# Linear attention: the summary's steps one slot later, and the keys' minimum on ScalarE

## The reference, cut to what matters

```
kvp = kv @ Wkv.T;  k, v = split(kvp)            # kv: 32 x 1500 x 256
q, k = phi(q), phi(k)                           # phi(x) = x + 1 if x > 0 else exp(x)
kv_summary = einsum('bhsd,bhse->bhde', k, v);   k_sum = k.sum(-2)
z = 1 / (einsum('bhld,bhd->bhl', q, k_sum)[..., None] + 1e-6)
attn = einsum('bhld,bhde->bhle', q, kv_summary) * z
out = attn * sigmoid(query @ Wg.T + bg) @ Wo.T
```

## Time and profile before

| | |
|---|---|
| median of three runs | 3338.97 us |
| the profiled execution's own time | 3340.39 us |
| its span in the profile | 3338.4 us |
| TensorE, VectorE, ScalarE, GpSimd busy over the span | 94%, 67%, 54%, 53% |
| mean granted TensorE clock | 0.97 of full |

### The profile page before, as it was taken

How to read it: one execution, slowest core, us unless ns; L and a number is a source line. 1 busy time by engine, 2 the same in 40 slices (tenths; PEclk the granted TensorE clock), 3 DMA queues, 4 the chain that set the end, 5 groups by cost and what they waited for, 6 DMA issues and landing times. The chain is left out here.

```text
span 3338.4 us, 65287 instructions
## 1 busy us (share of the span) xinstructions
PE 3125.9 (94%) x23304; PEld 2824.4 (85%) x23304; DVE 2222.3 (67%) x3434; ACT 1815.7 (54%) x3277; POOL 1770.9 (53%) x1890
## 2 busy tenths in 40 slices
PE   5999999996999999579999999999999999995999
PEld 4999999995999999558888888888888888884998
DVE  5888888884222222537877777787777777775554
ACT  3666666661323323146666666666666666662443
POOL 3877777771433433145565656555655565541332
PEclk9999999996999999789999999999999999996999
DMA  5544445421100100011111111011111111104000
GB/s 143 151 140 137 146 147 147 145 76 38 37 22 19 38 19 0 0 61 36 54 54 31 50 54 52 28 54 54 45 35 54 54 45 36 54 12 151 6 6 11
DMA packets 88460, 203.85 MB, mean 61 GB/s; under 512 B 25408, under 2 KB 64688, under 8 KB 83376
## 3 DMA queue, kind: packets, MB, share of 16 engines
q1 hardware_dynamic: 86288, 202.93, 19.4%
q10 hardware_dynamic: 2112, 0.12, 0.1%
HBM read 184.94 MB, written 14.42 MB: 60 GB/s over the span
## 5 line engine op out<-in xcount | busy, mean ns | idle before, releaser
L1437 DVE TENSOR_TENSOR a_probT<-a_p,a_probT 125x448 fp32r<-125x448 f32 x768 | 459.2, 617 | 155.1 <-ACT a_probT L1370 152.0
L1370 ACT CAST a_probT<-a_p 125x448 fp32r<-125x448 f32 x768 | 395.7, 537 | 255.8 <-PE a_p L1554 254.6
L1431 DVE TENSOR_REDUCE a_mxs<-a_s 112x1 f32<-112x1500 f32 x256 | 439.8, 1718 | 96.6 <-PE a_s L1542 93.0
L1569 PE MATMUL a_o<-a_probT,a_val 125*64 125x224 f32 x3072 | 473.3, 278 | 1.7 <-DVE a_probT L1437 0.9
L1554 PE MATMUL a_p<-ident,a_prob 112*125 112x112 f32 x3072 | 438.6, 274 | 2.5 <-DVE a_probT L1437 2.3
L1554 PEld LDWEIGHTS a_p<-ident,a_prob 112*125 112x125 f32 x3072 | 387.9, 188 | 43.7 <-issue 26.7
L1363 ACT ACTIVATE a_prob<-a_s,a_mxs 112x1500 f32<-112x1500 f32 x256 | 389.4, 1521 | 15.6 <-DVE a_mxs L1431 14.5
L1569 PEld LDWEIGHTS a_o<-a_probT,a_val 125*64 125x64 f32 x3072 | 338.0, 136 | 37.9 <-issue 24.5
L725 POOL TENSOR_TENSOR e_hT_lo<-e_h,e_hT_hi 128x448 fp32r<-128x448 f32 x144 | 167.7, 1165 | 353.3 <-ACT e_hT_hi L772 353.3
L438 POOL TENSOR_TENSOR l_rows_lo<-l_raw,l_rows_hi 125x512 fp32r<-125x512 f32 x192 | 267.1, 1391 | 163.6 <-ACT l_rows_hi L477 163.6
L1287 POOL TENSOR_TENSOR a_two<-a_picked 64x224 f32<-64x224 f32 x128 | 84.1, 657 | 434.3 <-DVE a_picked L1449 434.3
(11 more groups left out here) (279 smaller groups left out, 9266.1 us busy)
## 6 DMA issues: line engine op xcount, KB each, us to landing
l_rawT<-in_ctxT SPq DMA_DIRECT2D x32, 1500.0 KB, 6.2
a_rawT<-in_ctxT SPq DMA_DIRECT2D x32, 1500.0 KB, 6.2
l_raw<-in_ctx SPq DMA_DIRECT2D x32, 1344.0 KB
e_gu_in<-in_L_ffn_w_gate_up SPq DMA_DIRECT2D x8, 1024.0 KB, 4.9
W_hi<-w_out_hi SPq DMA_DIRECT2D x32, 192.0 KB, 2.4
W_lo<-w_out_lo SPq DMA_DIRECT2D x32, 192.0 KB, 2.4
l_raw<-in_ctx SPq DMA_DIRECT2D x32, 156.0 KB
e_down_in<-in_L_ffn_w_down SPq DMA_DIRECT2D x8, 512.0 KB, 5.8
```

The lines of the kernel that those rows point to most:

```text
L1370: act.copy(p_target(j, f, 0), p_source(i)).then_inc(p_hi[i], 1)
L1431: dve.tensor_reduce(mxs[:, j:j + 1], s_bank[0:TT, :, 0:GW], AX.XY, ALU.max, negate=True).then_inc(max_done, 1)
L1437: dve.tensor_tensor(p_target(j, f, 1), p_source(i), p_target(j, f, 0).bitcast(F32), ALU.subtract).then_inc(p_read[i], 1)
L1569: mm = pe.matmul(o_bank[0:2 * PW, at:at + 2 * TT], flat(val[:, ch, j, :, :]), flat(probT[j % 2][:, ch, :, :]), start=(ch == 0), stop=(ch = ...
```

## The change

Two things, both in `linear_attention`. The minimum moves from VectorE to ScalarE: expk = relu(-k), read from PSUM by ScalarE at the head of its slot (it waits for k and for the phif of two groups ago, as VectorE did), and the exponential is taken of -expk. ScalarE's stream of a slot is then relu, ctxT_hi, exp, rows_hi, phik_hi. And the once-a-batch steps for the summary move: on TensorE `gt` from slot 3 to 4, `kv` from 4 to 5, `numden` from slot 5 to slot 1 of the batch after; on ScalarE the GT copy and the scalings from slot 4 to 5; on VectorE `kv_copy` from slot 5 to slot 0 of the batch after, and `nd_use` from the end of a batch to slot 3 of the next, in front of the copies of G, which stay in slot 3. VectorE's loop is unrolled by one batch more at its start, and the steps of the last two batches are finished behind the loops.

```
 ScalarE
                 for g in range(NP):
+                    act.wait_ge(k_full, NP * b + g + 1)
+                    if g >= 2 or not first:
+                        act.wait_ge(phi_done, NP * b + g - 1)
+                    act.activation(expk[:, g % 2, :], k_bank[g % 2][0:CH, :], ACT.Relu, scale=-1.0).then_inc(min_done, 1)
...
-                    if g == 4 and not first:
+                    if g == 5 and not first:
                         act.wait_ge(gt_full, b)
                         act.copy(flat(GT[:, :, :]), gt_bank[:, :]).then_inc(gt_read, 1)
                         scale_queries(b - 1)
                     act.wait_ge(min_done, NP * b + g + 1)
-                    act.activation(expk[:, g % 2, :], expk[:, g % 2, :], ACT.Exp).then_inc(exp_done, 1)
+                    act.activation(expk[:, g % 2, :], expk[:, g % 2, :], ACT.Exp, scale=-1.0).then_inc(exp_done, 1)
 VectorE
+                    if g == 0 and not first and not known:
+                        kv_copy(b - 2)
+                    if g == 3 and not first and not known:
+                        nd_use(b - 2)
                     if g == 3 and not first:
                         g_copy(b - 1, 1 - u)
-                    if g == 5 and not first:
-                        kv_copy(b - 1)
-                    dve.wait_ge(k_full, NP * b + g + 1)
-                    if g >= 2 or not first:
-                        dve.wait_ge(phi_done, NP * b + g - 1)
-                    dve.tensor_scalar(expk[:, g % 2, :], k_bank[g % 2][0:CH, :], 0.0, None, ALU.min).then_inc(min_done, 1)
...
-                if not first:
-                    nd_use(b - 1)
...
+            kv_copy(B - 2)
             g_copy(B - 1, 1)
+            nd_use(B - 2)
             kv_copy(B - 1)
             nd_use(B - 1)
 TensorE
                     k_group(b, g, first)
-                    if g == 5 and not first:
-                        numden(b - 1)
                     if g >= 3:
                         g_group(b, u, g - 3, known)
                     elif not first:
                         g_group(b - 1, 1 - u, g + 3, False)
-                    if g == 3 and not first:
+                    if g == 1 and not first and not known:
+                        numden(b - 2)
+                    if g == 4 and not first:
                         gt(b - 1)
-                    if g == 4 and not first:
+                    if g == 5 and not first:
                         kv(b - 1, not known)
```

More of the change, by code:

```diff
@@ L528, in t_low, with batch @@
                                   ctxT.hi[:, :, cols].bitcast(F32), ALU.subtract).then_inc(t_lo, 1)
-            def batch(b, u, first=False, last=False):
+            def batch(b, u, first=False, known=False, last=False):
                 for g in range(NP):
+                    if g == 0 and not first and not known:
+                        kv_copy(b - 2)
+                    if g == 3 and not first and not known:
+                        nd_use(b - 2)
                     if g == 3 and not first:
                         g_copy(b - 1, 1 - u)
-                    if g == 5 and not first:
-                        kv_copy(b - 1)
-                    dve.wait_ge(k_full, NP * b + g + 1)
-                    if g >= 2 or not first:
-                        dve.wait_ge(phi_done, NP * b + g - 1)
-                    dve.tensor_scalar(expk[:, g % 2, :], k_bank[g % 2][0:CH, :], 0.0, None, ALU.min).then_inc(min_done, 1)
                     if g + 2 < NP:
@@ L555, in _ @@
             batch(0, 0, first=True)
-            with dve.Fori(0, B // 2 - 1) as i:
+            batch(1, 1, known=True)
+            with dve.Fori(1, B // 2 - 1) as i:
+                batch(2 * i, 0)
                 batch(2 * i + 1, 1)
-                batch(2 * i + 2, 0)
+            batch(B - 2, 0)
             batch(B - 1, 1, last=True)
+            kv_copy(B - 2)
             g_copy(B - 1, 1)
+            nd_use(B - 2)
             kv_copy(B - 1)
@@ L640, in _ @@
                 g_group(B - 1, 1, g, False)
+            numden(B - 2)
             gt(B - 1)
```

## The result

The changed kernel takes 3405.96 us (median of four runs, 3394.88 to 3413.3) beside 3338.64 before: ratio 1.0199, 95% interval 1.0166 to 1.0231. It is slower, as forecast, but by 67 us and not 33, and 1 us beyond the range. The profiled execution took 3413.3 us, 72.9 more than the one of before.

The account below looks back on a forecast made before the run. The chain phik_hi, phik_lo, ctxT_lo, phif was taken to bound the kernel, not TensorE. Slots summed to 22.47 us a batch against 21.44: +1.03 for 30 batches, 31, plus 1 and 0.5, giving 3372; range 3330 to 3405.

Parts of the forecast that it names:

- Slots 1 to 5: Distances between phifs within a linear attention batch, forecast at 3.26, 3.17, 5.26, 3.20 and 3.85 us.
- Slot 3 by the shut-out: VectorE's ctxT_lo, behind nd_use and G copies, waits until GpSimd's rows_lo ends at 4.04; slot 5.26 us.
- Case D: Within noise: ctxT_lo goes first in slot 3 (4.32), the rest as forecast; 3343 us, chance 0.14.
- TensorE stays busy enough that I cost its clock at nothing: In the linear attention stage, TensorE's granted clock was taken to add 0 us.
- the wait's growth: Sign in the profile after: TensorE's kv wait for GT up from 24 to about 60 us or more.
- k's lateness: Slot 0: k, queued behind kv, arrives at 0.95 where relu could start at 0.56: 0.38 us late.
- A: The forecast itself: slower, 3372 us, own range 3355 to 3392 (relu and slot 3 at bounds), chance 0.56.
- Every second batch 0.35 for TensorE's loop turn in slot 0: Slot 0, forecast 3.55 us, grows by 0.35 every second batch through TensorE's loop turn of 0.47.
- Rival C: Much slower: GpSimd's lag doesn't settle, ordinary slots take 3.6; +2.45 us a batch, 3412 us, chance 0.13.
- E: A table load at each change between Relu and Exp on ScalarE, 384 of 1.28 us; 3830 us, chance 0.01.
- B: Faster: ctxT_lo first in slot 3 (4.32), slot 0 3.2, slot 5 3.5, others 3.17; 3314 us, chance 0.16.
- The premise that the stage wasn't bound by TensorE: Linear attention: TensorE, though 93% busy, doesn't set the slot time; a chain of 3.15 us does.

Follow-up runs that it names:

- e2_relu_only: Kernel before the change with only the minimum moved to ScalarE as a Relu, the summary steps left where they were: 3330.76 us.
- f1_nd_split: Changed kernel with nd_use cut in two, its halves in slots 2 and 4 of VectorE: 3315.32 us.
- f2_gt_early: Changed kernel with ScalarE's GT copy behind rows_hi of slot 4 and the query scalings behind rows_hi of slot 5: 3335.35 us.
- f3_both: Changed kernel with nd_use cut into slots 2 and 4, GT copy behind rows_hi of slot 4, scalings behind rows_hi of slot 5: 3282.47 us.
- g2_fill6: Changed kernel with 6 idle products in TensorE's stream in front of kv, results unused: 3368.14 us.
- e4_rows_wait: Changed kernel with one added wait: in slot 3 GpSimd starts rows_lo only after VectorE's ctxT_lo: 3381.53 us.
- e3_shift_only: Changed kernel with the minimum back on VectorE behind the copies, so only the summary steps are moved: 3392.39 us.

## Why the prediction was wrong

- *Slots 1 to 5*: right, each within 0.2, by the chain over phik_hi, phik_lo and ctxT_lo. The Relu adds little in an ordinary slot (0 to 0.15 in e2_relu_only) and 0.48 in the one with the GT copy, as e2_relu_only shows for slot 4.
- *Slot 3 by the shut-out*: right (5.26 forecast, 5.20), and shown by a wait on GpSimd that shortens the slot. By the prediction's own rows the slot comes to 5.18: phif begins 0.07 before ctxT_lo's 4.57, as in the earlier trace rows, and the 5.26 leaves that out. Case D, ctxT_lo first, would have needed that wait.
- *The step that failed*: "TensorE stays busy enough that I cost its clock at nothing". The working had all of the idle stretch: kv at 2.18 of slot 5, TensorE done with its products before; it gave the wait's growth as a sign to look for, and k's lateness from it as 0.38. It didn't ask what 2.1 us of idle time do to an engine whose idle stretches before were 0.6 to 0.9. That term was 1.47 us in slot 0 of the median batch: 43 us between the profiled spans (3411.6 and 3368.7 filled), 37 between the medians. With it held at zero by filling, the kernel takes 3369.23, the forecast 3372. The range of A had no room for it either, and its ends don't follow from the bounds that it names: slot 3 at 4.32 alone gives 3344, and at 5.6 gives 3382.
- *Every second batch 0.35 for TensorE's loop turn in slot 0*: wrong, 0.17 a batch too much: the filled kernel's periods are 22.28 to 22.32, and k starts 0.91 to 0.92 behind kv in each. Why the 0.45 of before is gone stays open.
- *Rival C* had the right time, 3412, by the wrong mechanism: the lag of GpSimd settled at once, ordinary slots are 3.16. E is out: between the first phif and the last there is no table load. B's numbers needed two things that f1_nd_split and f2_gt_early had to bring about by other edits.
- *The premise that the stage wasn't bound by TensorE* was right: f2_gt_early took away the wait before kv and gained nothing on the kernel before; only with the chain on VectorE cleared as well, in f3_both, does TensorE run without bubbles.

At full clock the parts add up so: before 21.44, Relu alone 21.04, moved steps alone 22.04, both 22.29. The change's two halves don't help each other. The Relu's gain alone was in the slot of nd_use and the one behind it; with the moved steps, which put the copies beside nd_use, it gives 0.04 there and 0.40 in slot 4, and costs 0.48 in slot 5 and 0.20 in slot 1.

## What to carry to other kernels

Follow one period from result to result on all engines before believing a busy share: here the chain, not TensorE's 93%, set the time, and TensorE bound one slot of six. Then, for each wait that a move makes longer on TensorE, compare its length with the longest that the trace shows at full clock, and price the stretch behind it at half speed if it is well beyond; here that held in most batches, so it is a bound and not a sum. And a once-a-batch step belongs where its engine waits anyway, in pieces that fit that wait; two steps in one slot cost more than their sum when they push a VectorE operation with two inputs behind one of GpSimd's.

## What the runs showed of the hardware

- 2.1 us of idle TensorE once in 23.9 us, ahead of 4 us at a mean granted clock of 0.58; the same kernel with 6 or 16 products in the gap, at 1.00 throughout. Idle stretches of 1.4 (g2_fill6, f2_gt_early), 1.25 (e2_relu_only) and 0.83 (f1_nd_split) once a batch left the clock at 1.00. With 2.0 to 2.1 the fall is not in every batch: slot 0 varied between 3.57 and 5.04 in e4_rows_wait and between 3.57 and 4.71 in e3_shift_only. In the changed kernel it came later behind kv from batch to batch, then missed one batch.
- The cost came from what ran behind the gap: k, 12 products, took 2.7 us for 1.5, and ScalarE and VectorE waited for just that k.
- ctxT_lo on VectorE, begun while GpSimd's rows_lo ran, took 1.33 and ended 0.54 behind it; it took 0.67 once GpSimd waited for it.
